# Normalising and feeding the last feed-forward by batch: a two-layer attention and feed-forward kernel on one core

## The reference

```python
x = x + quantised_matmul(layernorm(x), ctx)                       # layer 0, attention
x = x + mx_ffn(layernorm(x), w_gate, w_up, w_down)                # layer 0, fp6 x fp4 feed-forward
x = x + attention(layernorm(x), ctx, ctx, mask, wq, wk, wv, wo)   # layer 1: 32 query heads, 8 key heads, rope
h = layernorm(x)                                                  # layer 1, feed-forward, width 1376
x = x + down_scale * ((silu(gate_scale * (h @ gate_w.T)) * (up_scale * (h @ up_w.T))) @ down_w.T)

def layernorm(x): return (x - mean(x)) / sqrt(var(x) + 1e-5)      # over the 512 values of a row
```

## Time and profile before

| | |
|---|---|
| time, median of 3 runs | 795.27 us (794.51 to 795.56) |
| the profiled execution: span from first to last instruction | 792.6 us |
| its own time | not recorded apart from the span; the median is 2.6 us above the span |
| TensorE busy, share of the span | 694.3 us, 88% |
| VectorE busy | 602.5 us, 76% |
| GpSimd busy | 497.3 us, 63% |
| ScalarE busy | 338.9 us, 43% |
| DMA, mean | 83 GB/s |

### The profile page before, as it was taken

One profiled execution on the slowest core, in us unless ns is written; L12 is line 12 of the kernel. 1 busy time (PEld: TensorE's weight loads), 2 busy tenths in 40 slices (PEclk: granted clock), 3 DMA queues, 4 the chain that ended last, 5 costly groups with the idle time before them and its releaser, 6 DMA issues.

```text
span 792.6 us, 10943 instructions
## 1 busy us (share of the span) xinstructions
PE 694.3 (88%) x3104; PEld 507.6 (64%) x3104; DVE 602.5 (76%) x1050; ACT 338.9 (43%) x654; POOL 497.3 (63%) x407
## 2 busy tenths in 40 slices
PE   4789638966676689999999999999999999599998
PEld 1344314433233567888888888888888888378886
DVE  6869999998878678888878878888888887631112
ACT  1323112212323267666666656666566665031111
POOL 0789897668424368675766667676767555517662
PEclk9979878978779899999999999999999999989999
DMA  8643432232140012212121221202111102202321
GB/s 336 249 142 124 133 119 74 73 106 66 54 146 26 26 54 94 67 54 67 40 93 39 80 66 40 93 26 93 44 62 58 36 27 93 62 19 81 118 79 53
DMA packets 38314, 65.67 MB, mean 83 GB/s; under 512 B 3344, under 2 KB 11664, under 8 KB 37264
## 3 DMA queue, kind: packets, MB, share of 16 engines
q1 hardware_dynamic: 38288, 65.36, 25.1%
HBM read 55.91 MB, written 9.44 MB: 82 GB/s over the span
## 4 chain that ended last, share of the span: by engine, by line
PE 64%; DVE 25%; issue 7%; POOL 2%; DMA 1%; ACT 1%; SPq 0%; POOLq 0%; DVEq 0%; ACTq 0%
PE ps L517 15%; PE ps L519 15%; PE ps L518 15%; PE ps L579 11%; PE ps L546 7%; DVE mx_q L1071 4%; DVE mx_m L1063 2%; DVE mx_q L1073 2%; DVE mx_amax L1048 2%; PE ps L474 2%; DVE mx_amax L1050 1%; DVE mx_raw L1069 1%; DMA k_scr<-k_cos 1%; DVE ctx_f L1000 1%; DVE k_cos L1079 1%
## 5 line engine op out<-in xcount | busy, mean ns | idle before, releaser
L897 POOL TENSOR_SCALAR prob<-prob,rinv 128x512 f32<-128x512 f32 x128 | 90.0, 703 | 122.1 <-DVE rinv L1203 122.1
L741 ACT ACTIVATE prob<-ps,nmax 128x512 f32<-128x512 f32 x128 | 88.4, 690 | 62.5 <-DVE nmax L1196 60.0
L579 PE MATMUL ps<-xt,wq_sb 128*128 128x512 f32 x384 | 106.4, 403 | 5.5 <-POOL wq_sb L888 2.2
L752 ACT CAST pT<-ps 128x512 fp32r<-128x512 f32 x128 | 75.1, 587 | 81.2 <-PE ps L546 80.3
L1196 DVE CUSTOM_DVE_ANT_0 ps<-ps,mask_sb 128x512 f32<-128x512 f32 x128 | 88.3, 690 | 18.2 <-PE ps L519 17.2
L1217 DVE TENSOR_TENSOR pT<-ps,pT 128x512 fp32r<-128x512 f32 x128 | 86.9, 679 | 4.7 <-ACT pT L752 1.7
L579 PEld LDWEIGHTS ps<-xt,wq_sb 128*128 128x128 f32 x384 | 73.9, 194 | 24.0 <-issue 4.6
L422 PE MATMUL ps<-ctxT,wk_sb 128*128 128x512 f32 x128 | 62.7, 647 | 18.2 <-DMA ctxT<-in_ctx_cols 10.5
L546 PE MATMUL ps<-idf,prob 128*128 128x128 f32 x512 | 76.6, 272 | 0.0
L546 PEld LDWEIGHTS ps<-idf,prob 128*128 128x128 f32 x512 | 64.0, 142 | 16.2 <-POOL prob L897 0.3
L432 PE MATMUL ps<-wv_sb,ctt 128*128 128x512 f32 x128 | 60.0, 624 | 16.3 <-DVE X L1036 16.3
(11 more groups left out here) (147 smaller groups left out, 1722.7 us busy)
## 6 DMA issues: line engine op xcount, KB each, us to landing
mx_raw<-in_mxw SPq DMA_DIRECT2D x8, 1024.0 KB, 6.2
wq_raw<-in_wq SPq DMA_DIRECT2D x32, 256.0 KB, 3.1
wo_raw<-in_wo SPq DMA_DIRECT2D x32, 256.0 KB, 2.6
k_scr<-k_cos SPq DMA_DIRECT2D x16, 256.0 KB, 6.3
v_scr<-v_st SPq DMA_DIRECT2D x16, 256.0 KB, 6.4
kr<-k_scr SPq DMA_DIRECT2D x16, 256.0 KB, 2.8
vr<-v_scr SPq DMA_DIRECT2D x16, 256.0 KB, 3.4
ffn_raw<-in_gate_w SPq DMA_DIRECT2D x11, 256.0 KB, 2.7
```

The lines of the kernel that those rows point to most:

```text
L579: last = mm(query_bank(H), wq_sb[:, par, l, k], xt[:, r, k], start=(n == 0), stop=(n == 11))
L741: nc.scalar.activation(prob[:, j], bank(j % 2), ACT.Exp, bias=nmax[:, j:j + 1], scale=-1.0, accum_out=rsum[:, j:j + 1]).then_inc(exps, 1)
L752: copy(pT[:, v % 2, 0, :, i * P:(i + 1) * P], bank(2 + i % 2).rearrange("p (k c) -> p k c", k=4)).then_inc(ph_ready, 1)
L897: nc.gpsimd.tensor_scalar(prob[:, i], prob[:, i], rinv[:, i:i + 1], 1.0, ALU.mult, ALU.mult).then_inc(probs, 1)
```

## The change

It does five things at the seam, and leaves the rest of the program alone.

- TensorE, unit 33: `last_pair` puts all four `project` steps of unit 30 ahead of the last two `weigh` groups of unit 31.
- VectorE: the statistics of each tile follow its last addition. `normalise` is cut into `spread` (aggregations and L980, L981) and `standardise` (the chain of nine and `xhat`). `spread(0, 2)` stands in unit 33 behind the second addition and ahead of `oT`'s low part. `standardise(0, 2)` stands at the head of unit 34, ahead of both additions of unit 31. `spread(2, 4)`, `batch_low(0)`, `standardise(2, 4)` and `batch_low(1)` follow.
- Transposes by batch (`turn_batch`): eight for each batch, into two banks that hold two blocks of 128 columns for two tiles each.
- Copies and subtractions for `xt_again` by batch (`batch_high`, `batch_low`): two of 512 columns for each batch, four in all as before.
- `gate_up_batch`: gate and up of slices 0 and 1 run on 256 columns of batch 0, then on those of batch 1, which makes 96 matmuls of 256 columns out of 48 of 512. Their sums are announced behind batch 1.

```diff
+            def last_pair(U, u, g):
+                weigh(U, u, 0, g)
+                for j in range(4):
+                    project(U, u, j)
+                weigh(U, u, 1, g)
+                weigh(U, u, 2, g)
             def unit(U, u, g):
+                if isinstance(U, int) and U == NUNIT + 1:
+                    last_pair(U, u, g)
+                    return
...
-            pe.wait_ge(proj_added, 2 * NUNIT)
-            turn_rows(3, ROW_BANKS[1])
+            def turn_batch(b):
+                for t in range(2 * b, 2 * b + 2):
+                    pe.wait_ge(ln_ready, 4 * 3 + t + 1)
+                for half in range(2):
+                    for k in range(2):
+                        for t in range(2):
+                            last = nc.tensor.transpose(bank(TURN_BANKS[b][half])[:, (2 * k + t) * P:(2 * k + t + 1) * P],
+                                                       xhat[:, 2 * b + t, (2 * half + k) * P:(2 * half + k + 1) * P], idf[:])
+                    last.then_inc(xh_turned, 1)
+            def gate_up_batch(c, b):
+                pe.wait_ge(fw_split, 2 * c + 1)
+                cols = slice(b * SEQ, (b + 1) * SEQ)
+                for m, done in ((0, g1_sums), (1, u1_sums)):
+                    for k in range(KD):
+                        if c == 0 and m == 0 and k % 2 == 0:
+                            pe.wait_ge(xtl_ready, KD + 2 * b + k // 2 + 1)
+                        last = three(bank(2 * m + c)[:, cols], [fw[:, c, m, s, k * P:(k + 1) * P] for s in range(2)],
+                                     [xt_again[:, s, k, cols] for s in range(2)], k == 0, k == KD - 1)
+                    if b == BATCH - 1:
+                        last.then_inc(done, 1)
...
-            gate_up1(0, 0)
-            gate_up1(1, 1)
+            for b in range(BATCH):
+                turn_batch(b)
+                for c in range(2):
+                    gate_up_batch(c, b)
             down1(0, 0)
...
+            def batch_high(b):
+                for half in range(2):
+                    act.wait_ge(xh_turned, KD + 2 * b + half + 1)
+                    copy(xt_again[:, 0, 2 * half:2 * half + 2, b * SEQ:(b + 1) * SEQ],
+                         bank(TURN_BANKS[b][half]).rearrange("p (k c) -> p k c", k=2)).then_inc(xth_ready, 1)
...
-            rows_high(1, xt_again)
+            batch_high(0)
+            batch_high(1)
...
+            def batch_low(b):
+                for half in range(2):
+                    dve.wait_ge(xth_ready, KD + 2 * b + half + 1)
...
             def unit(U, u, g):
+                if isinstance(U, int) and U == NUNIT + 2:
+                    standardise(0, 2)
                 for j in range(4):
...
                         tt(X[:, tile], bank(7), X[:, tile], ALU.add).then_inc(proj_added, 1)
-                        if isinstance(U, int) and U == NUNIT + 2 and i == 0:
-                            dve.wait_ge(proj_added, 2 * NUNIT - 1)
-                            for t in range(NT - 1):
-                                row_stats(t)
+                        if isinstance(U, int) and U > NUNIT:
+                            dve.wait_ge(proj_added, 2 * V + i + 1)
+                            row_stats(tile)
+                        if isinstance(U, int) and U == NUNIT + 1 and i == 1:
+                            spread(0, 2)
...
-            dve.wait_ge(proj_added, 2 * NUNIT)
-            row_stats(NT - 1)
-            normalise(0, NT)
-            rows_low(1, xt_again)
+            spread(2, NT)
+            batch_low(0)
+            standardise(2, NT)
+            batch_low(1)
             inter1(0, 0)
```

More of the change, by code:

```diff
@@ L35 @@
 CH = MXT * D
-ROW_BANKS = ([4, 5, 0, 1], [4, 5, 6, 7])
+ROW_BANKS = [4, 5, 0, 1]
+TURN_BANKS = ([6, 4], [5, 7])
 POOL_ADDS = (1, 2, 3, 4)
@@ L519, in three @@
                 return mm(out_ap, left[1], right[0], start=False, stop=final)
-            turn_rows(2, ROW_BANKS[0])
+            turn_rows(2, ROW_BANKS)
             def score(U, u, j, g):
@@ L627, in gate_up1 @@
                     for k in range(KD):
-                        if isinstance(c, int) and c == 0 and m == 0:
-                            pe.wait_ge(xtl_ready, KD + k + 1)
                         last = three(bank(2 * m + p), [fw[:, p, m, s, k * P:(k + 1) * P] for s in range(2)],
@@ L719, in _, with rows_high @@
             keep_inter(NT - 1)
-            def rows_high(turn, dst):
+            def rows_high():
                 for k in range(KD):
-                    act.wait_ge(xh_turned, 4 * turn + k + 1)
-                    copy(dst[:, 0, k], bank(ROW_BANKS[turn][k])).then_inc(xth_ready, 1)
+                    act.wait_ge(xh_turned, k + 1)
+                    copy(xt[:, 0, k], bank(ROW_BANKS[k])).then_inc(xth_ready, 1)
+            def batch_high(b):
[3 more added lines that the diff above has]
+                         bank(TURN_BANKS[b][half]).rearrange("p (k c) -> p k c", k=2)).then_inc(xth_ready, 1)
             act.wait_ge(kr_in[0], 16)
@@ L731, in _ @@
             nc.scalar.activation(rsum[:, 0:1], sc[:, 0:1], ACT.Exp, scale=0.0)
-            rows_high(0, xt)
+            rows_high()
             def exponent(U, u, j):
@@ L973, in normalise, with spread @@
             def normalise(lo, hi):
+                spread(lo, hi)
+                standardise(lo, hi)
+            def spread(lo, hi):
                 dve.wait_ge(ln_step, ln.n)
@@ L981, in normalise, with standardise @@
                 chain(ln, ts(r.bitcast(I32), var.bitcast(I32), -0.5, float(0x5F3759DF), ALU.mult, ALU.add))
+            def standardise(lo, hi):
+                var, r, step = var_eps[:, lo:hi], rstd[:, lo:hi], newton[:, lo:hi]
                 for _ in range(3):
@@ L1161, in _, with rows_low @@
             normalise(NT - 1, NT)
-            def rows_low(turn, dst):
+            def rows_low():
                 for k in range(KD):
-                    dve.wait_ge(xth_ready, 4 * turn + k + 1)
-                    tt(dst[:, 1, k], bank(ROW_BANKS[turn][k]), dst[:, 0, k].bitcast(F32), ALU.subtract).then_inc(xtl_ready, 1)
-            rows_low(0, xt)
+                    dve.wait_ge(xth_ready, k + 1)
+                    tt(xt[:, 1, k], bank(ROW_BANKS[k]), xt[:, 0, k].bitcast(F32), ALU.subtract).then_inc(xtl_ready, 1)
+            def batch_low(b):
+                for half in range(2):
+                    dve.wait_ge(xth_ready, KD + 2 * b + half + 1)
+                    part = (slice(2 * half, 2 * half + 2), slice(b * SEQ, (b + 1) * SEQ))
+                    tt(xt_again[:, 1, part[0], part[1]], bank(TURN_BANKS[b][half]).rearrange("p (k c) -> p k c", k=2),
+                       xt_again[:, 0, part[0], part[1]].bitcast(F32), ALU.subtract).then_inc(xtl_ready, 1)
+            rows_low()
             for b in range(BATCH):
```

## The result

The changed kernel takes 802.11 us (801.05 to 802.82) against 795.27, each the median of four executions; the ratio is 1.0087, with a 95% interval of 1.0074 to 1.0099. It is slower by 6.8 us; 802.5 was forecast, in a range of 798.5 to 806.5. The profiled span grew from 792.6 to 799.2 us.

A forecast was written before the change was run, and what follows sets the result against it. TensorE was taken to bound the kernel, the first matmul of down1(0) moving the end; its start went from 710.29 to 717.55 (+7.3 us), the span from 792.6 to 799.9, plus 2.6 gives 802.5, range 798.5 to 806.5.

The forecast's parts named there:

- Steps 1 and 2: Seam's start: project before weigh makes ScalarE's copy and GpSimd's splits 2.45 us later; spread(0, 2) is held, oT low ends 684.2.
- Step 3: standardise(0, 2) on VectorE: eleven instructions starting at 684.2 amid GpSimd's splits end at 694.35, against 687.0 alone.
- The open choice: In standardise(0, 2), two xhat around the last L942: both ahead end 693.1, one or both behind 694.4; 694.35 taken.
- Step 4: Unit 31's tile 2 addition waits until 694.3; TensorE idles 9.2 us, then its second sum takes 2.91 us at low clock.
- Step 5: Transposes and copies by batch: eight low-clock transposes end at 699.9, copies at 700.5, gate_up_batch starts at 700.9.
- Step 6: Batch 0's 256-column matmuls: 12 at 0.21 and 36 at 0.125 us end at 708.0.
- the low clock: Batch 0's matmuls: the clock stays low 8.3 us after work resumes, here to about 703.5.
- the bound of 0.22: Upper bound for one 256-column matmul: a transpose plus another 0.11 us gives 0.22.
- Step 7: Hand-over to batch 1: 1.9 us in which only transposes, ScalarE's copy and VectorE's subtraction run; batch 1 begins at 709.9.
- Step 8: down1(0) waits for L1250, 4.43 us after slice 0's sums, and starts at 717.55, +7.3 us against 710.29.
- the last rival: Batch matmuls of 256 columns save nothing, at 0.22 us each: +13 us, 808 to 809; chance 0.05.
- The rival that nothing is held up: VectorE passes freely beside GpSimd's splits at the seam; down1(0) starts at 707.0: -3.3 us, 792.0; chance 0.10.

The follow-up runs named there:

- Experiment 4: The kernel before with only the new order of the last project and weigh calls: 796.90 us, ratio 1.0030.
- Experiment 1: The changed kernel with GpSimd's weight splits held back until batch 0's two normalised tiles are written: 793.47 us, ratio 0.9987 to the kernel before.
- Experiment 5: The kernel before with only gate and up of slices 0 and 1 made in two halves of 256 columns: 796.46 us, ratio 1.0024.
- experiment 6: The changed kernel with GpSimd's subtraction for slice 2's weights held until slice 0's low part is made, later slices likewise: 800.11 us, ratio 1.0071.
- experiment 7: The changed kernel with both the first splits and slice 2's subtraction on GpSimd held back: 791.41 us, ratio 0.9959 to the kernel before.
- experiment 3: The kernel before with GpSimd's splits held back until three of its four xhat are written: 791.27 us, ratio 0.9961.

## Why the prediction was right

It was right in sign and mechanism, and close in size. The working predicted 41.03 us for the seam, and 39.70 were measured, so the sum was 1.3 us too long. That the median came out within 0.4 us of the forecast is in part luck: the seam began 0.53 later, and the 2.6 us added for the time outside the span were 1.85 in the changed kernel's profiled execution (801.05 against 799.2), which was itself the fastest of the four. With the seam's later start of 0.53 taken off, step by step:

- **Steps 1 and 2** hold to within 0.1 us: the second sum begins 2.44 us behind the first (2.45 in the text), the splits begin at 682.73 (682.2 + 0.53), L1024 and L1025 are held (0.45 and 0.55) and `oT` low ends at 684.67 (684.2 + 0.53). Experiment 4 shows that part alone.
- **Step 3**, the core, came as written: one instruction at the end of each GpSimd instruction and one more in each gap. The open choice, the pair of `xhat` around the last L981, fell as chosen, behind it, but both were through by 694.57 instead of 694.9, 0.7 us after L981. Experiment 1 shows the cause.
- **Step 4**: the low-clock sum took 698.15 - 695.23 = 2.92 us (2.91 in the text). The idleness was 8.1 us, not 9.2: the first sum already ran partly at the low clock and ended 0.7 later, and the second began 0.4 earlier.
- **Step 5** holds to 0.3 us: `gate_up_batch` starts at 701.17 (700.9 + 0.53).
- **Step 6** was mis-sized by 1.2 us, nearly the whole error of the sum. The term that failed is the low clock: the 8.3 us for which it stayed low after work resumed before were carried over, and 3.8 us were measured. The clock fell at 685.4 and not at 691, and was back at 699.0, ahead of batch 0's matmuls. Windows of 1 us of the changed kernel, columns as in rows 2:

```profile
685.00:686.00 1.00, 1.00 (x4) 0.78 (x4) 1.00 (x1) 0.00 (x0) 1.00 (x1) 0.70 0.00 0
...
698.00:699.00 1.00, 1.00 (x6) 1.00 (x5) 0.78 (x2) 0.00 (x0) 0.00 (x0) 0.50 0.00 0
699.00:700.00 1.00, 0.53 (x5) 0.29 (x3) 0.93 (x4) 0.96 (x2) 0.00 (x0) 0.97 0.00 0
```

  So all 48 ran at 0.12 us, 5.8 us in place of 7.0. The 0.125 us taken for a matmul measured 0.120, and the bound of 0.22 was far off. The estimate of 0.109 us, worked out from the Trainium skill's figure ("TensorE: Matmul & The Clock Gate", section "Back-to-back issue gap"), is 9% below the rows.
- **Step 7**: 709.08 - 706.99 = 2.09 us, 1.9 in the text.
- **Step 8** came as written: slice 0's sums end at 712.19, L1307 ends 4.41 us later (4.43 in the text) after 2.85 us beside L974, and TensorE waits 1.69. Experiment 5 shows the wait without the rest of the change, and experiments 6 and 7 show it gone.

Three readings of the working were off without moving the result. The spacing of 512-column matmuls is 5.44 / 24 = 0.227 us and not 0.2275. The 0.163 for 384 columns is the spacing of starts (eight in 1.31 us); the 1.47 us of rows 14 include the last one's length. And the range leaves out the whole of the last rival, 808 to 809, and not half of it.

The parts do not add up to the whole: by the medians the order alone costs 2.5 us, the halves alone 2.0, and the change 6.8, although it also starts the feed-forward on batch 0 alone. Holding the splits back is worth 7.3 us of seam in the changed kernel (39.70 to 32.40) and 3.1 in the kernel before. With one hold each, the kernel before (0.9961) is ahead of the changed one (0.9987). The rival that nothing is held up forecast 792.0; experiment 1, which makes that case for batch 0 alone, gave 793.5. There the chain of batch 1 meets the splits (its nine take 5.9 us, 693.20 to 699.09, instead of 1.7), and `down1(0)` still waits for its held subtraction.

What stays open is when exactly the clock falls. Experiments 1 and 7 have nearly the same waits of TensorE up to the first feed-forward matmul (1.57, 1.61 and 2.35 us), and in the profiled executions the clock was low for some 3.4 us in the one and at 1.00 all through the seam in the other. What a fall costs depends on what waits there. In experiment 6 it made batch 0 last 1.5 us longer. In experiment 1 it cost nothing by the start of batch 1, since TensorE had to wait for batch 1's `xhat` in either case. No experiment held the clock fixed.

## What to carry to other kernels

When work on VectorE is moved in time, look at what GpSimd runs at that time, and price a chain of small dependent instructions by GpSimd's instructions and not by their own 0.16 us: each one of GpSimd's lets one of them through. Ask then which instruction stands behind the chain in VectorE's queue; here it was an addition that freed the bank TensorE needed, and eleven instructions, nine of them tiny, left TensorE idle for 8.1 us. A wait of one line on the engine with slack, GpSimd, gained 0.4% in the kernel before. The restructuring lost 0.9% without such waits, gained 0.1% with one, 0.4% with two, and 0.5% with three more moves.

## What the runs showed of the hardware

- An instruction of VectorE on 128x2 numbers took up to 2.20 us instead of 0.16 beside a GpSimd TENSOR_TENSOR of 128x1024, while those that read PSUM and one SBUF operand kept their 0.69. So the engines' streams do not meet at semaphores only: here they waited for each other where no semaphore stood. The Trainium skill ("SBUF — State Buffer", section "Who interferes with whom") has the exclusive lock, and these traces agree; what they add is that a queue of GpSimd instructions let exactly one of the small chained instructions through at each end, and one more in each gap of 0.08 us. The `xhat` of 128x512 that started in such a gap was held up all the same (1.58 us).
- The hold goes both ways. Beside VectorE's tiny instructions GpSimd's hardly stretched (2.34 to 2.38 us for L974 with and without a waiting VectorE). But in experiment 3 a subtraction of 128x512 with both inputs in SBUF got in between two of GpSimd's, and the second of these took 1.06 us instead of 0.62, 1.64 for the pair instead of 1.20:

```profile
702.29 1.64 POOL L933 TENSOR_SCALAR fw<-ffn_raw 128x512 fp32r<-128x512 f32 x2
702.47 0.98 DVE L1251 TENSOR_TENSOR int1s<-int,int1s 128x512 fp32r<-128x512 f32 x1 [0.69 <-ACT int1s L805]
```

- Matmuls of 256 columns in fp32r follow each other at 0.120 us at 2.4 GHz and at 0.21 at 1.2 GHz, those of 512 at 0.227 and 0.43: half the width took 53% of the time at 2.4 GHz, although each matmul has a weight load of its own.
- The clock fell after idle stretches of very different length. In the kernel before it stayed at 2.4 GHz through 1.4 and 0.8 us and fell 4.7 us into the 6.65 us ahead of the transposes. In the changed kernel it was at 0.50 from 685.4 on, when TensorE, idle from 682.50 to 684.73, was already at work again; in experiment 7 it stayed at 1.00 through 2.35 us.
